# Two-layer transformer on one core: in layer 0, exponentials of neighbouring steps added in pairs before the ones' matmuls

## The reference, cut to what matters

```python
Q = _split_heads(x, H)                    # 16 heads of 8
K = _split_heads(x @ Wk + bk, H)
V = _split_heads(x @ Wv + bv, H)          # 16 heads of 32
scores = jnp.einsum('bhqd,bhkd->bhqk', Q, K) + mask      # causal
attn = jax.nn.softmax(scores, axis=-1)
o = jnp.einsum('bhqk,bhkd->bhqd', attn, V)
return x + jax.nn.gelu(o, approximate=False) @ Wf + bf
```

## Time and profile before

| | |
|---|---|
| median of 3 runs | 2563.59 us |
| the profiled execution | 2583.99 us, span 2582.2 us |
| granted TensorE clock, mean | 0.867 of full speed |
| busy, share of the span | TensorE 86%, VectorE 58%, ScalarE 52%, GpSimd 32% |

### The profile page before, as it was taken

How to read it: one execution, slowest core, us unless ns; L and a number is a source line. 1 busy time by engine, 2 the same in 40 slices (tenths; PEclk the granted TensorE clock), 3 DMA queues, 4 the chain that set the end, 5 groups by cost and what they waited for, 6 DMA issues and landing times. The chain is left out here.

```text
span 2582.2 us, 30828 instructions
## 1 busy us (share of the span) xinstructions
PE 2217.8 (86%) x11109; PEld 873.0 (34%) x11109; DVE 1486.7 (58%) x3043; ACT 1343.8 (52%) x1923; POOL 833.9 (32%) x909
## 2 busy tenths in 40 slices
PE   6799976779999998778999999777899999877789
PEld 2233432234433342223443344222343334322243
DVE  6562556856556266675656445677565635577552
ACT  2345447962244635795225553688423454378922
POOL 1112125533411313562331221365142122146534
PEclk7899977879999986588999998767899999766889
DMA  5200231004310023100520022110051002401013
GB/s 145 67 15 18 67 99 36 1 1 119 101 28 2 21 78 83 36 1 13 143 72 20 2 66 80 36 36 1 23 156 42 20 2 83 98 9 27 1 53 88
DMA packets 67850, 128.38 MB, mean 50 GB/s; under 512 B 11397, under 2 KB 24837, under 8 KB 63077
## 3 DMA queue, kind: packets, MB, share of 16 engines
q1 hardware_dynamic: 67696, 126.40, 17.9%
HBM read 109.99 MB, written 15.20 MB: 48 GB/s over the span
## 5 line engine op out<-in xcount | busy, mean ns | idle before, releaser
L1281 DVE TENSOR_REDUCE mx<-ps 128x1 f32<-128x512 f32 (+3 forms) x992 | 612.5, 655 | 373.8 <-PE ps L620 241.3
L1029 ACT ACTIVATE pr<-ps 128x1024 f32<-128x1024 f32 (+3 forms) x672 | 515.0, 804 | 404.3 <-PE ps L690 403.7
L690 PE MATMUL ps<-qop,kop 75*128 75x512 bf16 (+7 forms) x1344 | 407.6, 367 | 123.1 <-DVE wb L1343 41.5
L617 PE MATMUL ps<-kop,qop 72*128 72x512 bf16 (+6 forms) x1248 | 425.4, 374 | 92.1 <-DVE mx L1281 69.7
L1572 POOL TENSOR_SCALAR_AFFINE_SELECT pr<-pr 128x512 f32<-128x512 f32 x224 | 145.5, 649 | 730.9 <-ACT pr L1029 730.1
L736 PE MATMUL ps<-pr,vt 128*32 128x512 f32 (+3 forms) x2688 | 340.4, 584 | 8.2 <-POOL pr L1572 7.6
L1090 ACT ACTIVATE pr<-ps 128x512 f32<-128x512 f32 x224 | 133.8, 597 | 337.6 <-PE ps L846 273.7
L617 PEld LDWEIGHTS ps<-kop,qop 72*128 72x128 bf16 (+1 forms) x1248 | 128.1, 105 | 424.9 <-DVE mx L1281 256.1
L690 PEld LDWEIGHTS ps<-qop,kop 75*128 75x128 bf16 (+1 forms) x1344 | 121.6, 104 | 361.7 <-ACT pr L1029 117.9
L856 PE MATMUL ps<-pr,w_down 128*128 128x512 f32 x384 | 196.7, 599 | 4.1 <-POOL pr L1563 4.1
L843 PE MATMUL ps<-hT,w_gate 128*128 128x512 f32 x384 | 196.2, 592 | 0.2 <-DVE on L1508 0.2
(11 more groups left out here) (316 smaller groups left out, 3153.0 us busy)
## 6 DMA issues: line engine op xcount, KB each, us to landing
wb<-gates_scratch SPq DMA_DIRECT2D x192, 256.0 KB, 3.4
kop<-kparts_scratch SPq DMA_DIRECT2D x32, 576.0 KB
qop<-qparts_scratch SPq DMA_DIRECT2D x96, 192.0 KB
on<-hmax_scratch SPq DMA_DIRECT2D x8, 1024.0 KB, 5.7
kparts_scratch<-on SPq DMA_DIRECT2D x12, 256.0 KB, 2.9
qparts_scratch<-on SPq DMA_DIRECT2D x12, 256.0 KB, 4.9
qparts_scratch<-wb SPq DMA_DIRECT2D x12, 192.0 KB
kparts_scratch<-wb SPq DMA_DIRECT2D x12, 192.0 KB
```

The source lines that it names most:

```text
L617: mm = pe.matmul(o, qop[0:k, slot(l, u), j, qb * P:(qb + 1) * P], kop[0:k, slot(l, u), j, k0:k0 + wd], start=True, stop=not diag)
L690: mm = pe.matmul(o, kop[0:k, slot(l, u), 2 * pair + j, kb * P:(kb + 1) * P], qop[0:k, slot(l, u), 2 * pair + j, q0:q0 + wd], start=True, s ...
L1029: nc.scalar.activation(pr[:, g % 3, 2 * pair:2 * pair + 2, o0:o0 + wd], ps[:, bank:bank + 2, o0:o0 + wd], ACT.Exp).then_inc(a.exps, 1)
L1281: ins_ = nc.vector.tensor_reduce(mx[:, nth(l, u) % 2, j0:j0 + heads, qb, col % 2], ps[:, bank, 0:heads * wd].rearrange("p (j n) -> p j n", ...
```

## The change

In layer 0 a pair of neighbouring steps (0 and 1, 2 and 3, and so on) shares its ones' matmuls. When both steps' exponentials (cut, where they lie on the diagonal) are there and the even step's values are through, VectorE adds the odd step's into the even step's buffer for two heads, GpSimd for the other two. TensorE runs four ones' matmuls over the even step's width. Exponentials go round through five buffers (three of `pr` and two of `wb`). The ones' matmuls of a pair stand behind the values of the odd step that follows it. VectorE's addition stands in an even step amid that step's side work, GpSimd's behind the cut of the pair's odd step. `sums_out` and `scale_out` stand two steps later than before, at steps 6 and 2. Five set-up semaphores are shared with others.

```diff
+        def probs(l, g):
+            if l:
+                return pr[:, g % 3]
+            return (pr[:, 0], pr[:, 1], pr[:, 2], wb[:, 0], wb[:, 1])[g % RING0]
+
+        def pair_halves(k, heads):
+            _, _, q0, wd, _ = STEPS[(2 * k + 1) % NS]
+            o0 = q0 % CH
+            return [probs(0, 2 * k + i)[:, heads, o0:o0 + wd] for i in range(2)]
...
                             pe.wait_ge(a.o_out, out_before(u, c))
-                            if l == 0:
-                                pe.wait_ge(a.s_out, NC * u + c)
...
-                    if l == 0:
-                        for j in range(4):
-                            mm = pe.matmul(ps[32 * j:32 * j + 32, 5, o0:o0 + wd], ones32[:],
-                                           pr[:, g % 3, j, o0:o0 + wd], start=kb == 0, stop=last,
-                                           tile_position=(0, 32 * j))
-                        mm.then_inc(a.pv, 1)
+                    mm.then_inc(a.pv, 1)
+
+                def sums(k):
+                    u, s = divmod(2 * k, NS)
+                    c, kb, q0, wd, _ = STEPS[s]
+                    o0 = q0 - c * CH
+                    pe.wait_ge(a.added[0], k + 1)
+                    pe.wait_ge(a.added[1], k + 1)
+                    if kb == 0 and k:
+                        pe.wait_ge(a.s_out, NC * u + c)
+                    for j in range(4):
+                        mm = pe.matmul(ps[32 * j:32 * j + 32, 5, o0:o0 + wd], ones32[:],
+                                       probs(0, 2 * k)[:, j, o0:o0 + wd], start=kb == 0, stop=kb == 4 * c + 2,
+                                       tile_position=(0, 32 * j))
+                    mm.then_inc(a.sums, 1)
...
+                    if l == 0 and p % 2 and 3 <= p:
+                        sums((p - 3) // 2)
...
+                    sums(NS * UNITS // 2 - 1)
                     pe.wait_ge(a.exps, 2 * NS * UNITS)
...
-                    act.wait_ge(a.pv, NS * u + 4 + 8 * c)
+                    act.wait_ge(a.sums, (NS * u + 4 + 8 * c) // 2)
...
-                        if g >= 3:
+                        if l == 0 and g >= RING0:
+                            act.wait_ge(a.sums, (g - RING0) // 2 + 1)
+                        elif l and g >= 3:
                             act.wait_ge(a.pv, g - 2)
...
-                        if s == 4:
+                        if s == 6:
                             sums_out(u, 0)
-                        if s == 0 and u:
+                        if s == 2 and u:
                             sums_out(u - 1, 1)
...
+                def add_pair(k):
+                    even, odd = pair_halves(k, slice(0, 2))
+                    if STEPS[(2 * k + 1) % NS][4]:
+                        dve.wait_ge(a.cut, diagonals(2 * k + 2))
+                    else:
+                        dve.wait_ge(a.exps, 2 * (2 * k + 2))
+                    dve.wait_ge(a.pv, 2 * k + 1)
+                    nc.vector.tensor_tensor(even, even, odd, ALU.add).then_inc(a.added[0], 1)
...
-                    first = len(SIDE[l, more][p]) // 2 if shift != NOBODY else 99
+                    adding = l == 0 and p and p % 2 == 0
+                    first = len(SIDE[l, more][p]) // 2 if shift != NOBODY or adding else 99
                     for x in SIDE[l, more][p][:first]:
                         side_job(*x)
...
+                    if adding:
+                        add_pair(p // 2 - 1)
                     for x in SIDE[l, more][p][first:]:
                         side_job(*x)
...
+                pool.wait_ge(at[0].pv, 2 * k + 1)
+                nc.gpsimd.tensor_tensor(even, even, odd, ALU.add).then_inc(at[0].added[1], 1)
...
                 cut(0, g)
-                if g % NS == 4:
+                if g % 2:
+                    add_pair(g // 2)
+                if g % NS == 6:
                     scale_out(g // NS, 0)
-                if g % NS == 0 and g:
+                if g % NS == 2 and g >= NS:
                     scale_out(g // NS - 1, 1)
```

More of the change, by code:

```diff
@@ L16 @@
 HYP_RING = 5
+RING0 = 5
 PAIRS = 3 * HD * 3
@@ L452, in __init__ @@
                 self.pv = sem(n + "pv")
+                if l == 0:
+                    self.added = [sem(n + "added_dve"), sem(n + "added_pool")]
+                    self.sums = sem(n + "sums")
                 self.o_out = sem(n + "o_out")
@@ L736, in values @@
                         mm = pe.matmul(ps[32 * j:32 * j + 32, 4, o0:o0 + wd], vt[:, kb, 32 * h:32 * h + 32],
-                                       pr[:, g % 3, j, o0:o0 + wd], start=kb == 0, stop=last,
+                                       probs(l, g)[:, j, o0:o0 + wd], start=kb == 0, stop=last,
                                        tile_position=(0, 32 * j))
-                        if l and j == 3:
-                            mm.then_inc(a.pv, 1)
-                    if l == 0:
-                        for j in range(4):
-                            mm = pe.matmul(ps[32 * j:32 * j + 32, 5, o0:o0 + wd], ones32[:],
-                                           pr[:, g % 3, j, o0:o0 + wd], start=kb == 0, stop=last,
-                                           tile_position=(0, 32 * j))
-                        mm.then_inc(a.pv, 1)
+                    mm.then_inc(a.pv, 1)
[12 more added lines that the diff above has]
+                    mm.then_inc(a.sums, 1)
                 def hyp_values(k):
@@ L1026, in std_exp @@
                         act.wait_ge(a.scores, 2 * g + pair + 1)
-                        if g >= 3:
+                        if l == 0 and g >= RING0:
+                            act.wait_ge(a.sums, (g - RING0) // 2 + 1)
+                        elif l and g >= 3:
                             act.wait_ge(a.pv, g - 2)
-                        nc.scalar.activation(pr[:, g % 3, 2 * pair:2 * pair + 2, o0:o0 + wd],
+                        nc.scalar.activation(probs(l, g)[:, 2 * pair:2 * pair + 2, o0:o0 + wd],
                                              ps[:, bank:bank + 2, o0:o0 + wd], ACT.Exp).then_inc(a.exps, 1)
@@ L1569, in cut @@
                 if diag:
-                    past = pr[:, g % 3, :, q0 - c * CH:q0 - c * CH + P]
+                    past = probs(l, g)[:, :, q0 - c * CH:q0 - c * CH + P]
                     pool.wait_ge(at[l].exps, 2 * (g + 1))
@@ L1573, in cut, with add_pair @@
                                             channel_multiplier=-1).then_inc(at[l].cut, 1)
+            def add_pair(k):
+                even, odd = pair_halves(k, slice(2, 4))
+                if STEPS[(2 * k + 1) % NS][4]:
+                    pool.wait_ge(at[0].cut, diagonals(2 * k + 2))
+                else:
+                    pool.wait_ge(at[0].exps, 2 * (2 * k + 2))
+                pool.wait_ge(at[0].pv, 2 * k + 1)
+                nc.gpsimd.tensor_tensor(even, even, odd, ALU.add).then_inc(at[0].added[1], 1)
             def hyp_cut(k):
@@ L1835, in next_batch @@
             nc.all_engine_barrier(sems_to_clear=range(first_sem, last_sem + 1))
-        s_mod = ctx.enter_context(nc.semaphore("s_mod"))
-        s_silu = ctx.enter_context(nc.semaphore("s_silu"))
-        s_mm = ctx.enter_context(nc.semaphore("s_mm"))
+        s_mod = tables
+        s_silu = sq_ready
+        s_mm = ss_ready
         s_ready = ctx.enter_context(nc.semaphore("s_ready"))
-        s_consts = ctx.enter_context(nc.semaphore("s_consts"))
+        s_consts = t_col
         with nc.Block() as block:
```

## The result

The changed kernel takes 2603.6 us, the kernel before 2563.0 us in the same comparison: a ratio of 1.0162, 95% interval [1.0134, 1.0190]. A second comparison, on another occasion, gave 2597.78 against 2564.86, 1.0143 [1.0110, 1.0177]. The change makes the kernel slower by some 33 to 41 us; the prediction had 2567 and a range that ended at 2600. (One execution of 3069 us, at a granted clock of 0.618, was a disturbed one and is left out.) The profiled execution of the changed kernel took 2600.52 us.

The account below looks back on a forecast made before the run. It took VectorE, then a transfer, to set a unit's length from step 7's end, with TensorE and VectorE near balance before. Gains of 12.0 us and a clock loss of 15.6 gave +3.6, 2567 us, range 2532 to 2600.

Parts of the forecast that it names:

- What the change removes: Ones' matmuls on TensorE: 3.56 us a unit, 57.0 us in 16 units, as the ceiling of the gain.
- Step 8: VectorE's addition of pair 6 and 7 delays `maxima`, `max` and the next scores: 1.24 us lost in each of three units.
- Steps 4 to 7: Shorter or absent ones' matmuls, less what step 6's addition takes back: a gain of about 1.8 us a unit.
- Steps 0 to 3: Middle units: savings offset by a 0.9 us stall for step 3's cut; VectorE's addition meeting GpSimd's product costs 0.4 us.
- The last unit: No reductions, but GpSimd's cuts behind its additions and an addition on the stage's tail: a gain of 0.6 us a batch.
- The first unit: No chain from a unit before: a gain of 1.9 us a batch, 2.0 with the lower clock at its start.
- The clock: TensorE stands still 2.3 us in step 9 and its clock falls: 1.3 us at each of 12 edges, 15.6 us.
- Rival 2: Clock loss at unit edges costs the full 2.6 us each: 2583 us, or 2599 with steps 2 and 3; chance 0.34.
- Rival 3: VectorE and GpSimd meet in every pair and cuts slip: 4 to 10 us more, 2571 to 2577; chance 0.10.

Follow-up runs that it names:

- e4: Changed kernel with GpSimd's addition of steps 8 and 9 moved behind step 10's cut: 2577.39 us.
- e3: Changed kernel with GpSimd's additions alone cut to 8 columns a head, VectorE's kept whole: 2571.5 us.
- e1: Changed kernel with both engines' additions cut to 8 columns a head, all waits and matmuls kept: 2541.86 us.
- e8: Changed kernel with three moves: GpSimd's addition of steps 8 and 9, its product, and VectorE's additions of steps 6 and 8, all later: 2554.48 us.
- e10: Changed kernel with VectorE's additions alone moved: step 6's behind its fourth reduction, step 8's into step 9 behind the mask row's copy: 2591.71 us.
- e11: Changed kernel with GpSimd's product of the unit before alone moved from step 2 to behind step 3's cut: 2591.32 us.
- e7: Changed kernel with nine matmuls of zeros filling TensorE's hole in step 9, ahead of the `max` matmul: 2593.98 us.
- e9: e8 with VectorE adding all four heads in a batch's last unit and GpSimd none: 2547.92 us.
- e12: e9 with no addition for the last pair at the end of a batch's stage, its ones running over both buffers: 2549.14 us.

## Why the prediction was wrong, step by step

**What the change removes** held: 62 us of busy time against a ceiling of 57.0 worked out from starts.

**Step 8** failed, and it is the largest miss of the prediction. It counted what stands between the last reductions and `max` as the addition, 1.24 us, and the ones that go, 0.89, for a hole of 2.3. The addition took 1.22 us in its place, but the hole is 2.93. What it missed is the other engine: GpSimd's addition of pair 8 and 9 falls on `maxima` and holds a copy, or the cast behind it, to its end. e4 prices that at 1.00 us of hole and some 20 us of time, of the 33 between the forecast (+3.6) and the mean measured (+36.8); the sum had nothing for it. The prediction did price such a meeting, from the earlier trace rows, but looked for it where two additions with two inputs meet, at step 2, and not at the short copies and casts on the path. Alone, VectorE's addition is worth 0.9 us of hole (e3 against e1, e4 against e8), less than 1.24, in part since the copy ahead of `max` then takes 0.175 us and not 0.33 or 0.38.

The trace of before had shown such a meeting, ahead of the stage of the third batch: VectorE, then GpSimd.

```profile
1321.43 1.19 DVE L1150 CAST nmp<-nm 128x32 bf16<-128x32 f32 x1
```

```profile
1321.31 1.27 POOL L1563 TENSOR_TENSOR pr<-pr,wb 128x512 f32<-128x512 f32 x1 [1.92 <-DVE pr L1508]
```

This cast, 0.18 us at the unit edges, takes 1.19 and ends 0.04 us behind GpSimd's addition. The copy's 0.38 us at the edges of before are of the same kind: in the fourth batch's second unit it ended at 2051.42, 0.03 behind a cut of 0.63.

The Trainium skill, page "SBUF — State Buffer", section Who interferes with whom, has this too: copies and casts on VectorE can enter a mode in which they share a port pair with GpSimd, and then the second to come waits for the whole of the first. The prediction cited an earlier section of that page, and for instructions with two inputs alone. The copies of 1.17 us and casts of 1.78 that end 0.03 and 0.04 us behind GpSimd's addition agree.

**Steps 4 to 7** promised 1.8 us a unit. Neither profile shows a middle unit that is shorter. One part is seen: step 6's addition, 1.24 us in the forecast, took 1.65 (2052.19 to 2053.84), beside GpSimd's product from 2051.49 to 2052.75; in e10, behind the fourth reduction, it took 1.22. How much of the 1.8 was reached before the hole took it back isn't settled.

**Steps 0 to 3** were right in detail: the values of step 3 wait for the cut, 0.89 us against a forecast of 0.9, and the product beside VectorE's addition took 1.68 us instead of 1.27, 0.41 against 0.4. But the prediction let what goes in steps 0 and 1 pay for the stall, and came out even. e11 takes stall and meeting away; its stage is 14 to 17 us shorter, over 1 us in each of 12 units, so it wasn't even.

**The last unit** was to gain 0.6 us a batch with its tail. With the tail it lost 8 to 10 us in four batches (127.7 and 126.3 to 135.5 and 136.8): last units some 2, the end 7. That VectorE's addition of the last pair is on the tail was named; that the ones of the pair ahead are there too was not. In the units themselves the prediction had GpSimd's cuts behind its additions of 1.81 us, but not that these are held by VectorE's addition of the same pair: 2.58 and 3.41 us, and with either engine's additions short or gone the last units take 102 to 105 us.

**The first unit**'s 2.0 us a batch didn't come: 182.3 and 181.0 became 183.0 and 179.1. It has the same edge.

**The clock** was right in kind. The half speed stands behind the unit edges in all batches, at 10 to 12 edges of 12. The price was 15.6 us; e7 gives 9 to 15 of the stage, which is near it. Rival 2 named a time close to the measured one, 2599, by a price of 2.6 us an edge and a clock lost in steps 2 and 3 too. The clock was lost there in the last units, but an edge costs 1 to 2 us by e7, and e4 brings over half of the loss back by moving one addition: that the times are close is luck. Rival 3, held additions and slipping cuts, had the right family, at 4 to 10 us, and about that is what it costs in the last units; the one meeting that it lacked, with the copy of `maxima`, cost some 20.

## What to carry to other kernels

Before more work on SBUF is given to GpSimd, list every short VectorE instruction on a path that falls in its span, copies and casts of a few elements among them, and price each at what is left of the GpSimd instruction, not at its own length. When two delays meet on one path, taking away one shows little in the wait (e10, 0.3 us of hole for 1.2 moved) until the other is gone (0.9, e4 to e8); a one-at-a-time experiment on the wrong one looks like a refutation. And two engines that start on the same pair at once hold one another: split between them, the last units' additions took longer (114.6 us for the units of e8) than on VectorE alone (102.0 in e9). Work taken off the engine with the greatest share was worth at most 19 us of 57 here (e1), and 14 of them remained where the added instructions stood behind the reductions and one engine alone added in the last units (e9, 2547.92 us).

## What the runs showed that was not expected

A copy of 128 x 16 float32 took 0.175 us undisturbed, 0.38 in the kernel before, behind the rest of a cut, and 1.17 beside a GpSimd addition of 1.80 us; a cast of 128 x 32 0.18 and 1.78. The reductions out of PSUM that ran beside the same addition kept their 0.68 us. GpSimd was held in turn: its addition of 1024 elements a partition took 3.41 us where VectorE's had begun 0.05 us before it, and 2.37 beside a short one. The clock didn't follow the hole alone: at 1.04 to 1.06 us it fell within 7 us behind `max` at 2, 1, 6 and 6 edges of 12 in e1, e8, e9 and e12, and at 2.93 us it held at two edges of the first profile. A hole makes the fall likely; where it falls isn't settled by these runs.
